# A graph layer with correction rows: loads, rank network and light tiles of both ends put in another order

## The reference

```python
msg = x[src]
agg = jax.ops.segment_sum(msg, dst, num_segments=n)
deg = jax.ops.segment_sum(jnp.ones((src.shape[0],), x.dtype), dst, num_segments=n)
mean = agg / jnp.maximum(deg, 1.0)[:, None]
h = mean @ W_l + b + x @ W_r
y = h * jax.nn.sigmoid(h)
out = (x + y - mean(x + y)) / sqrt(var(x + y) + 1e-5)   # along each row
```

## Time and profile before

| | |
|---|---|
| median of 3 runs (lowest, highest) | 1617.12 us (1616.44, 1617.76) |
| the profiled execution | 1616.76 us |
| its span, first to last instruction | 1615.0 us |
| PE busy | 1574.8 us, 98% |
| DVE busy | 1408.7 us, 87% |
| ACT, POOL busy | 1028.8 us, 947.9 us |
| chain that ended last | PE 95%, DVE 2%, DMA 1%, issue 1% |

### The profile page before, as it was taken

The page is one execution under the profiler, slowest core; times in us unless marked ns, Lnnn a source line. Parts: engine busy times, 40 slices in busy tenths (PEclk is TensorE's granted clock), DMA queues, the critical chain, the costliest instruction groups (busy, mean ns, idle before and its releaser), DMA issues.

```text
span 1615.0 us, 24709 instructions
## 1 busy us (share of the span) xinstructions
PE 1574.8 (98%) x7886; PEld 1311.1 (81%) x7886; DVE 1408.7 (87%) x2174; ACT 1028.8 (64%) x1433; POOL 947.9 (59%) x1089
## 2 busy tenths in 40 slices
PE   7998899999999999999999999999999999999996
PEld 5887688888888888888888888888888888888884
DVE  7988799999996888888888888888888888888886
ACT  4443343333335777777777777777777777777775
POOL 6446566666654665655566556665556656666563
PEclk9999999999999999999999999999999999999998
DMA  5456589888884676766667666666667666677674
GB/s 186 147 163 189 170 262 266 263 265 262 266 250 150 220 230 201 237 211 216 223 208 227 218 213 219 219 221 213 222 212 228 217 210 231 205 228 221 205 235 152
DMA packets 204245, 350.52 MB, mean 217 GB/s; under 512 B 37020, under 2 KB 51126, under 8 KB 204117
## 3 DMA queue, kind: packets, MB, share of 16 engines
q1 hardware_dynamic: 156135, 274.22, 51.6%
q0 software_dynamic: 46944, 74.22, 16.7%
q10 hardware_dynamic: 1038, 0.50, 0.1%
HBM read 288.78 MB, written 139.67 MB: 265 GB/s over the span
## 4 chain that ended last, share of the span: by engine, by line
PE 95%; DVE 2%; DMA 1%; issue 1%; SPq 0%; ACT 0%; POOL 0%; POOLq 0%; DVEq 0%
PE pH L473 81%; PE pT L567 9%; PE pT L541 3%; PE pT L482 1%; DMA light_h<-in_x 0%; DVE w_sum L799 0%; DVE w_sum L794 0%; DVE sums L923 0%; DMA light_x<-in_x 0%; PE pH L500 0%; PE pH L503 0%; DVE stats L1001 0%; SPq L246 0%; DVE row_mask L790 0%; DVE Z L794 0%
## 5 line engine op out<-in xcount | busy, mean ns | idle before, releaser
L473 PE MATMUL pH<-ws_hi,x_hi 128*128 128x512 f32 x1564 | 629.1, 402 | 0.0
L473 PE MATMUL pH<-ws_hi,x_lo 128*128 128x512 f32 x1564 | 611.4, 391 | 0.0
L473 PE MATMUL pH<-ws_lo,x_hi 128*128 128x512 f32 x1564 | 609.4, 390 | 0.0
L383 POOL DMA_INDIRECT cor<-correction_rows,node_idx x347 | 366.2, 1055 | 313.3 <-ACT cor L671 229.8
L708 ACT ACTIVATE x_hi<-pT 128x1024 fp32r<-128x1024 f32 x174 | 178.1, 1024 | 272.7 <-PE pT L567 272.7
L473 PEld LDWEIGHTS pH<-ws_hi,x_lo 128*128 128x128 f32 x1564 | 293.6, 188 | 63.3
L473 PEld LDWEIGHTS pH<-ws_lo,x_hi 128*128 128x128 f32 x1564 | 294.7, 188 | 54.5
L473 PEld LDWEIGHTS pH<-ws_hi,x_hi 128*128 128x128 f32 x1564 | 294.2, 188 | 54.5 <-issue 0.3
L986 DVE TENSOR_TENSOR Z<-pH,cor 128x1024 f32<-128x1024 f32 x174 | 212.5, 1221 | 100.4 <-PE pH L473 94.6
L717 ACT ACTIVATE O<-Z,shift,rstd 128x512 f32<-128x512 f32 x347 | 261.9, 804 | 3.2 <-DVE shift L1011 3.2
L1001 DVE BATCH_NORM_STATS2 stats<-Z 128x6 f32<-128x512 f32 x347 | 221.4, 680 | 0.0
(11 more groups left out here) (132 smaller groups left out, 1785.6 us busy)
## 6 DMA issues: line engine op xcount, KB each, us to landing
X<-in_x SPq DMA_DIRECT2D x173, 512.0 KB, 4.2
out<-O SPq DMA_DIRECT2D x173, 512.0 KB, 5.1
correction_rows<-c_out SPq DMA_DIRECT2D x98, 256.0 KB, 4.2
light_x<-in_x SPq DMA_DIRECT2D x66, 256.0 KB, 5.0
light_h<-early_product SPq DMA_DIRECT2D x44, 256.0 KB, 5.7
out<-light_o SPq DMA_DIRECT2D x44, 256.0 KB, 5.5
join_row<-joined SPq DMA_DIRECT2D x98, 64.0 KB, 4.1
light_h<-in_x SPq DMA_DIRECT2D x22, 256.0 KB, 2.9
```

The costliest lines, as they stand in the source:

```text
L383: g.indirect_dma_start(out=out_, out_offset=None, in_=table, in_offset=bass.IndirectOffsetOnAxis(ap=idx, axis=0), bounds_check=bound, oob_ ...
L473: last = mm(ps, a[:, k], w[:, k], start=(n == 0), stop=(n == len(terms) - 1))
```

## The change

Nothing is added to or taken from the arithmetic; instructions stand elsewhere.

* SP: x tile 1 is loaded after the first pair of weight blocks, not after all four. Early tiles from 28 (LATE) on are loaded into the eight slots of X, six tiles ahead, each with its own semaphore, and not two ahead into `e_x`.
* PE: the carry, the counts and the loop merge each stand one early tile later. The transposes of the last early tile and the first turn stand ahead of the product of tile 42. The marking matmuls stand after edge tile 4.
* DVE: loop_row(5) stands ahead of the wait for the carry. Seven column rounds, not six, stand ahead of the first scan; one more ahead of the first split_sums, and the last behind it. find_nodes stands after edge tile 6, not 2.
* ACT: the product of early tile 42 is kept after the first round_sums.
* All: the light tiles from 35 on take three pairs each, the first two steps in one pair, and are through before the last pairs. DVE's and ACT's work after the last pairs is reordered.

```diff
+    LATE = 28
+        def early_x(t):
+            if t < LATE:
+                return e_x[t % 2][:], early_x_in[t % 2], 16 * (t // 2 + 1)
+            return X[:, t % 8 // 2, t % 2], late_x_in[t % 8], 16 * ((t - LATE) // 8 + 1)
-        def light_tail(light, first, end):
-            for k in range(first, end):
-                light(k // 4, k % 4)
+        def lights(light, t):
+            every_fourth = 4 * (EARLY - 9)
+            if t < every_fourth:
+                light(t // 4, t % 4)
+            else:
+                l, s = divmod(t - every_fourth, 3)
+                l += EARLY - 9
+                if l <= EARLY:
+                    if s == 0:
+                        light(l, 0)
+                    light(l, s + 1)
...
             def load_early(t, q, u):
-                b = u % 2
-                wait(sp, early_transposed, t - 1)
-                sp.dma_start(e_x[b][:], x[bass.ts(t, P), :]).then_inc(early_x_in[b], 16)
+                tile, arrived, _ = early_x(t)
+                wait(sp, early_transposed, t - 1 if t < LATE else t - 7)
+                sp.dma_start(tile, x[t * P:(t + 1) * P, :]).then_inc(arrived, 16)
             def move_early(t, q, u):
-                shifted(t, q, u, 2, EARLY, load_early)
+                if t + 2 < LATE:
+                    single(t + 2, load_early)
+                if t + 6 == LATE:
+                    sp.wait_ge(rows_moved, 2)
+                if LATE <= t + 6 < EARLY:
+                    single(t + 6, load_early)
                 shifted(t, q, u, -1, EARLY, store_early)
             for k in range(K):
                 sp.dma_start(wl_raw[:, k], w_l[k * P:(k + 1) * P, :]).then_inc(weights_in[k], 16)
                 sp.dma_start(wr_raw[:, k], w_r[k * P:(k + 1) * P, :]).then_inc(weights_in[k], 16)
-            single(1, load_early)
+                if k == 0:
+                    single(1, load_early)
...
-            single(4 * FIND_ROUND + 1, early_tile)
+            peeled(4 * FIND_ROUND + 1, 4 * FIND_ROUND + 3, early_tile)
             pe.wait_ge(carry_ready, 1)
...
-            peeled(4 * FIND_ROUND + 2, 4 * FIND_ROUND + 4, early_tile)
+            peeled(4 * FIND_ROUND + 3, 4 * FIND_ROUND + 5, early_tile)
             pe.wait_ge(t_deg, 1)
...
-            single(4 * FIND_ROUND + 4, early_tile)
+            single(4 * FIND_ROUND + 5, early_tile)
             pe.wait_ge(loops_moved, 1)
...
+            single(EARLY - 1, transpose_early)
             single(0, turn)
-            single(EARLY - 1, early_tile)
+            single(EARLY - 2, early_matmuls)
             single(1, turn)
+            single(EARLY - 1, early_matmuls)
...
+                if t == 4:
+                    mark_rows_before()
...
             single(0, round_sums)
+            single(EARLY - 2, keep_early)
             single(1, carry)
...
-            loop_cols(0, col_bits - 3)
+            loop_cols(0, col_bits - 2)
             single(0, scan)
-            loop_cols(col_bits - 3, col_bits)
+            single(2, subtract)
+            loop_cols(col_bits - 2, col_bits - 1)
+            single(0, split_sums)
+            loop_cols(col_bits - 1, col_bits)
             v.memset(upto[:, 0:1], 0.0)
...
-                if fixed(t) and t == 2:
+                if t == 6:
                     find_nodes()
```

More of the change, by code:

```diff
@@ L174, in gnn_layer @@
         stored = [sem(f"stored{b}") for b in range(2)]
-        early_x_in = [sem(f"early_x_in{b}") for b in range(2)]
+        early_x_in, late_x_in = [sem(f"early_x_in{b}") for b in range(2)], [sem(f"late_x_in{b}") for b in range(8)]
         early_stored = [sem(f"early_stored{b}") for b in range(2)]
@@ L330, in move @@
                 shifted(t, q, u, -3, NP, store_out)
-                light(q, u)
+                lights(light, t)
             peeled(0, NP, move)
-            light_tail(light, NP, 4 * EARLY)
             for t in range(NP - 3, NP):
                 single(t, store_out)
-            light_tail(light, 4 * EARLY, 4 * EARLY + 4)
             sp.wait_ge(light_stored, 16 * EARLY)
@@ L477, in transpose_early @@
             def transpose_early(t, q, u):
-                b, used = ring(q, u, 2)
-                pe.wait_ge(early_x_in[b], 16 * (used + 1))
+                b = u % 2
+                tile, arrived, count = early_x(t)
+                pe.wait_ge(arrived, count)
                 wait(pe, early_copied, t - 1)
                 for k in range(K):
-                    last = nc.tensor.transpose(pT[b][:, 0, k * P:(k + 1) * P], e_x[b][:, k * P:(k + 1) * P], eye)
+                    last = nc.tensor.transpose(pT[b][:, 0, k * P:(k + 1) * P], tile[:, k * P:(k + 1) * P], eye)
                 last.then_inc(early_transposed, 1)
@@ L748, in node_pair @@
                 shifted(t, q, u, -1, NP, silu)
-                light(q, u)
+                lights(light, t)
                 shifted(t, q, u, -3, NP, normalise)
             peeled(0, NP, node_pair)
+            single(NP - 1, silu)
             single(NP - 3, normalise)
-            single(NP - 1, silu)
-            light_tail(light, NP, 4 * EARLY)
             single(NP - 2, normalise)
             single(NP - 1, normalise)
-            light_tail(light, 4 * EARLY, 4 * EARLY + 4)
         @block.vector
@@ L891, in _ @@
             loop_row(4)
+            loop_row(5)
             dve.wait_ge(carry_col, 1)
@@ L1055, in node_pair @@
                 shifted(t, q, u, -2, NP, make_shift)
-                light(q, u)
-            peeled(0, NP, node_pair)
+                lights(light, t)
+            peeled(0, NP - 1, node_pair)
+            single(NP - 2, add_cor)
+            single(NP - 3, moments)
+            single(NP - 2, residual)
+            lights(light, NP - 1)
             single(NP - 1, add_cor)
+            single(NP - 3, make_shift)
             single(NP - 2, moments)
             single(NP - 1, residual)
+            single(NP - 1, moments)
             single(NP - 2, make_shift)
-            single(NP - 1, moments)
-            light_tail(light, NP, 4 * EARLY)
             single(NP - 1, make_shift)
-            light_tail(light, 4 * EARLY, 4 * EARLY + 4)
 _INS = ["x", "src", "dst", "L0_gnn_W_l", "L0_gnn_W_r", "L0_gnn_b"]
```

26 lines of the change are left out of this document (12 added, 14 removed).

## The result

The changed kernel takes 1627.89 us (median of 6 runs, 1626.99 to 1629.84), the kernel before beside it 1616.78 us (6 runs, 1616.12 to 1617.81). The ratio is 1.0069, 95% interval [1.0056, 1.0082]: **slower by 11 us, where 13.8 us of gain were forecast**. The profiled execution has a span of 1626.6 us, before 1615.0.

What follows compares the result with a forecast made beforehand. PE, busy throughout both long stages, bounds the kernel, so only its idle times and low-clock stretches could be won. The terms sum to 13.8 us off 1616.76, 1603.0; with 0.36 for the median, 1603.3 us, range 1600.0 to 1607.5.

Steps and rivals of the forecast that it cites:

- Light tiles in threes: Node pairs, one light tile per three pairs: DVE's work fits, PE has more in hand; 0 us.
- The start: PE's second tile: x tile 1 loaded earlier lets PE begin it near 16.95, not 17.76; 0.8 us, bounds 0 and 1.2.
- The carry: PE's wait for the carry: an early tile now stands ahead, so all of it goes; 1.5 us.
- The load of tile 41: PE's wait for a late-issued load: fetched six tiles ahead it can't be late; 2.25 us.
- The loop merge: PE's 2.1 us wait for DVE at the merge shrinks to 0.4; gain 1.7 us, bounds 1.0 and 2.1.
- The clock at the merge: Merge matmuls: with so short a wait PE's clock stays up; 1.75 us, bounds 0 and 1.75.
- POOL's term: Tiles 32 to 39: POOL nearly full, PE waits that let it catch up gone; -0.3 us, bounds 0 and -1.5.
- The entry: Entry into the edge tiles: waits of 2.8 and 1.35 us replace one of 5.54; gain 1.4 us.
- The marking clock: Marking matmuls after edge tile 4, no longer behind a wait, run at full clock; 1.37 us, bounds 0 and 1.37.
- find_nodes: Edge tiles: its 1.5 us of DVE still costs PE 1.35 us two tiles later; gain 0, bound +1.35.
- The clock falls again: Rival: PE's low clock returns at entry or merge; once costs 1.7 us, 1605.0, twice 1606.7; chance 0.17.
- The tail: Behind the last matmul: without the light tile last, the store is issued earlier; 3.3 us, bounds 2.3 and 3.8.

Runs made afterwards that it cites:

- threes_all_rstd_first: The changed kernel with POOL's rstd of the pair and all its light steps ahead of its two gathers: 1608.06 us, ratio 0.9948.
- threes_light_behind: The changed kernel with ACT's light steps of the threes behind its ordinary normalise in the same pair: 1611.36 us, ratio 0.9956.
- entry_order_of_before: The changed kernel with ACT's light normalise one pair later, plus the earlier kernel's DVE order at the edge-tile entry: 1610.87 us, ratio 0.9947.
- all_mends: The changed kernel with ACT's light normalise one pair later, threes_all_rstd_first's edits, find_nodes after edge tile 5 and entry_kept_busy's matmuls: 1604.76 us, ratio 0.9913.
- threes_rstd_first: The changed kernel with POOL's rstd of the pair, but not the light rstd, ahead of its gathers: 1625.16 us, ratio 1.0057.
- entry_kept_busy: The changed kernel with ACT's light normalise one pair later, plus useless matmuls (eight, six) in PE's two waits at the edge-tile entry: 1603.21 us, ratio 0.9917.

## Why the prediction was wrong

**The step that failed** is the line "Light tiles in threes", priced at 0 and measured at -24.1 us. Its first half, that DVE's work fits (17.2 us of busy time a group), holds: DVE has 145.48 us in 8.5 groups, 17.1 each. The second half does not: "PE has more in hand: x_hi and x_lo of a pair are made while it multiplies the pair before, 5.5 us". That adds two durations and takes both engines to be free when the transposes are done. ACT is not: in its order x_hi stands behind the light normalise and the ordinary one and the reset of cor, and those behind a shift that DVE makes last in the same pair. The wait was in the text, as a rival with a chance of 0.04 and a price of 2 us a group, 1621.3 us. Its size was about right (2.8 us a group measured, in eight to nine groups), and so was the first half of its mechanism, the late normalise and the late x_hi; its second half, light_add waiting for its load, did not happen. That the size came out is in part luck: the half that was right makes up a sixth of the loss. What I had "against" it, PE's 3 us in hand, was never followed through ACT's order, which was written out in the diff. And the return path, reset, gather, rstd, shift, was not seen at all; by threes_all_rstd_first it makes up some five sixths (PE's loss is 4.2 us without it and 24.1 with it). The Trainium skill (DMA: Bandwidth & Descriptors, "Anatomy of one DMA"), from which the prediction has 2.6 us for a light load beside the row's 5.7, gives that fit for DMAs issued by GpSimd. SP issues these loads, and nothing rested on the figure.

**The start**, 0.8 forecast: tile 1's matmuls start near 17.0 as forecast; the next transposes stand at 16.52 against 17.40, 0.9. The transposes of tile 1 had moved much more, against

```profile
7.49 1.12 PE L499 MATMUL pT<-eye,light_h 128*128 128x128 f32 x4 [2.17 <-DMA light_h<-in_x]
10.87 0.76 PE L489 MATMUL pH<-ws_hi,x_hi 128*128 128x512 f32 x1 [2.26 <-DVE ws_lo L804]
```

so the weights bind tile 0, as the text said. For tile 1 the reason given was not the one that held: its x_lo was ready at 16.28 and not at 16.8, and PE was still at tile 0, whose matmuls start 0.43 us apart up to 16.52 (0.23 later on). The right 17.0 is luck in that part. **The carry**: no wait, 1.5 as forecast. **The load of tile 41**: no wait, 2.25 as forecast.

**The loop merge**, 1.7 forecast, 1.2 measured (the earlier trace rows against the first row):

```profile
141.68 1.16 PE L520 MATMUL pH<-eye,wr_raw 128*128 128x128 f32 x8 [0.78 <-DVE wr_raw L923]
...
165.51 0.66 PE L561 MATMUL pT<-eye,diff 128*128 128x128 f32 x4 [2.02 <-DVE diff L937]
167.65 0.77 PE L489 MATMUL pH<-wl_hi,s_hi 128*128 128x512 f32 x1 [1.48 <-DVE s_lo L954]
```

DVE was to be done at 141.1 and was at 141.63. It began the last three row rounds 0.9 us earlier (128.80, before 129.70); of those 0.7 went, since four of POOL's x_lo now fall beside that work, before three, and each makes a DVE instruction beside it longer, mostly by 0.9 to 1.1 us. (The cast into wr_raw took 1.63 us, before 0.69, but the instruction ahead of it, which had met the same x_lo before, took 1.05 and not 1.97.) **The clock at the merge** stayed up (1.16 us for the first eight matmuls, before 2.06; 1.89 for all sixteen, before 3.52): 1.6, forecast 1.75. Together with POOL's term, -0.3, which can't be told from the rest, the text had 7.7 us up to the last early tile, and it is 7.4.

**The entry**: forecast were 2.8 us of wait before edge tile 0 and 1.35 before tile 1. Measured are 2.2 and 1.7, both before tile 0 with a turn between, and 0.3 before tile 1. The sum is right and the split is not: DVE's s_lo of tile 0 ended at 167.50 and not at 165.8, since the merge ended 0.6 later than reckoned and rounds 1 to 6 took 16.65 us and not 15.7, with five of POOL's x_lo beside them and not four; and the second wait is short only because tile 0 ran at the low clock in its place (4.15 us from its first matmul to the next turn). The 5.54 us of the kernel before was read 0.25 too short as well: four transposes are shown with 0.60 us although the next matmul starts after 0.35. **The marking clock**: the marking runs at the full clock (1.31 us, before 2.74), 1.4 gained. The clock fell at the entry instead, which the rival "The clock falls again" had at 1.7 and a chance of 0.17; in this kernel it cost nothing (43.99 us from the merge to the marking, 43.98 with the clock kept up), as the argument against that rival had it. From the last early tile to the twelfth turn 1.8 us were gained, 2.8 forecast: the term of the entry, 1.4, gave 0.4, and what it lacks is DVE's one x_lo more. **find_nodes**: 0, as forecast, with the reason confirmed: a tile earlier 1.3 us are saved. **The tail**: 3.3 forecast, 3.7 measured, inside the bounds. The last ACT instructions of the changed kernel, the third of which starts at about 1620.8, 7.1 us behind the last matmul's start (6.5 to 7.5 forecast):

```profile
1619.42 2.22 ACT L743 ACTIVATE O<-Z,shift,rstd 128x512 f32<-128x512 f32 x3 [1.57 <-DVE shift L1036]
...
1621.66 0.33 SPq L317 DMA_DIRECT2D out<-O  x1
```

So of 13.8 us forecast, 12.5 came (8.8 and 3.7), and one term of nought took 24.1. With that term mended by one moved instruction the kernel is at 0.9929 of before, 1605.3 us on the scale of the 1616.78 of the result, inside the range that was given.

**What stays open.** A single wait of DVE of 1.0 to 3.2 us near 350 us shows in four of the profiles (the changed kernel, threes_light_behind, entry_order_of_before, all_mends) and in none of the others. DVE stands before its c_out there while PE's matmuls for it are long done, and PE then waits for diff. By the kernel that instruction waits for one thing more, the store of the c_out two tiles before, which leaves this store as the likely cause; that is inferred, and no run was made for it. Nor is it known why the low clock at the entry ended sooner in some profiles than in others.

## What to carry to other kernels

Where steps are moved closer together, the sum of busy times per engine says only that the work fits. Follow, for each instruction that now waits for another engine in the same round, what stands behind it in its own queue and who waits for that, until the path comes back to the start: here a wait of 3.6 us on ACT, behind which x_hi and a reset stood, became 2.8 us of PE in three pairs, with every engine under 92%. The same wait with a fourth pair in each group cost 2.0 us in all: the path closes on itself only where no slack is left in the round. Such a wait is mended by its place: put it behind what others need, or one round later.

A trial that cuts one link must show in the waits that it is cut; judged by the time alone, threes_rstd_first would have cleared the link that made most of the loss.

A difference of 1 us between two profiles is not the edit's until profiles that share the code in question are laid beside it: here they differ by up to 1.3 us at the entry.

## What the runs showed of the hardware

* **The clock behind short waits.** PE's clock was granted at the lower level (1.2 GHz) for most of edge tile 0 (0.66 in a window of 4.0 us from 167.7), behind waits of 2.2 and 1.7 us with four transposes between them. It had not fallen behind the 0.93 us at the merge. Fourteen matmuls of no use in the waits at the entry held it at 1.00 (entry_kept_busy, all_mends). The length of a wait alone does not decide: near 350 us two kernels have the same wait at the same turn. Behind the one below (entry_order_of_before) the granted clock is 0.50, behind that of all_mends (350.79, above) it stays at 1.00.

```profile
354.70 1.12 PE L561 MATMUL pT<-eye,diff 128*128 128x128 f32 x4 [2.61 <-DVE diff L940]
```

* **What a low clock costs depends on what PE waits for next.** At the entry it was 0 to 1.3 us, by whether it ended before DVE's next s_lo was there.
* **DVE's instructions beside POOL's x_lo.** Beside the row and column rounds each x_lo (1.3 to 1.8 us on POOL) made a DVE instruction longer, mostly by 0.9 to 1.1 us. Which one it is depends on the order. The same instruction in the kernel before and in the changed one, where the cast behind it took 0.69 and 1.63 us:

```profile
139.16 1.97 DVE L799 COPY_PREDICATED w_sum<-row_mask,w_sum 128x764 int32<-128x764 int32 x1
```

```profile
138.91 1.05 DVE L823 COPY_PREDICATED w_sum<-row_mask,w_sum 128x764 int32<-128x764 int32 x1
```

Where a reordering gains less than a microsecond on DVE, one such meeting more takes it.
